# A graph layer on one core: edge lanes of 100000, an uneven last pair, last stores lane by lane, x loaded earlier, norm operands in PSUM

## The chip, the cores and the metric

One core of a Trainium2 chip runs the whole kernel. The time is the device time of one execution in microseconds (us), the median of several runs. Lower is better.

## The reference, cut to what matters

```python
h = maximum(layernorm(x), 0)                      # x: 12500 nodes x 32
e = concat([h[src], h[dst], edge_attr], -1)       # 400000 edges x 96, dst is sorted
v = relu(e @ W1 + b1) @ W2 + b2                   # 96 -> 64 -> 32
x_cand = segment_max(v, dst, num_segments=12500)
out = x + maximum(x_cand, h)
```

## The kernel before, in words

The 400000 edges are cut into A = 4 lanes. A lane lies on 32 partitions. A block is 32 x 16 = 512 edges of one lane, and a step of the main loop (a pair, `j`) takes two blocks of every lane. There are `PAIRS` = 98 pairs, which is 98 x 1024 = 100352 edges a lane (`LEN`), somewhat more than a quarter of the edges. So the lanes overlap: the first three start at equal distances (`STEP`), the last one at `E - LEN`. A load of edge attributes, first rows or mask is therefore two DMAs, one for three lanes and one for the fourth (`lanes_of`, `row_view`, L287 to L298, L356 to L366).

Ahead of the main loop ("the start", up to about 300 us) the kernel normalizes x (L799 to L820, on VectorE, with one square root on ScalarE), writes h to memory, searches the first edge of every node (TensorE L668 and L670, ScalarE L597), splits a table of h, and scatters h to the first edge of each node.

In a pair, 12 of each 16 rows of `h[src]` are fetched by GpSimd's indirect DMAs, one DMA for 128 rows: 24 gathers a pair (`gather_row`, L490). The other 4 of 16 are looked up by TensorE with one-hot matrices (L689). One-hots are made by VectorE (L927) and ScalarE (L615, L620). TensorE then runs the two layers (`layer_one`, `layer_two`, L704 to L727). VectorE turns inputs around (L958, L964, L969), spreads first rows over the edges with a scan (L973), takes the running maximum with a second scan (L984), turns it (L988), and SP stores it to `run_max` (L429).

What sets the order:
- SP's queue is in order. For a pair it waits and issues: edges for `j+2`, first rows for `j+2`, picks for `j+3`, every seventh pair the indices, then the mask for `j+2`, then the store of `j` (`feed`, L431 to L454). The wait ahead of the indices is on the gathers of the last pair of the running set of seven (L447).
- GpSimd gathers seven pairs ahead at most. Two gathers form a burst, and burst `b` of pair `j` waits until TensorE has used `(j - 5) * 13 + b` tiles (L507 to L511).
- VectorE's queue is in order: in `pair` it masks, turns edges, scans, makes one-hots, and last it turns the gathered rows of the next pair (`turn_src`, L954).

After the last pair SP loads x again, waits for all stores, and loads a row for each lane that carries a maximum over its border. GpSimd waits for all stores too, and then gathers one row of `run_max` for each node: 98 gathers (L560). VectorE joins them with h and x, and SP writes the output (L475).

Of the kernel before, what the change touches and what calls it, by code (L numbers as in the profile page):

```python
# [7 lines left out]
ALU = mybir.AluOpType  # L8
# [5 lines left out]
P = 128  # L14
# [5 lines left out]
A = 4  # L20
# [9 lines left out]
LEN = 2 * PAIRS * BLK  # L30
assert LANES == F == 32 and A * LEN >= E and PAIRS % (2 * AHEAD) == 0
STARTS = [a * ((E - LEN) // (A - 1)) for a in range(A - 1)] + [E - LEN]
STEPS = [STARTS[a] - STARTS[a - 1] for a in range(1, A)]
assert all(0 < s < LEN for s in STEPS)

STEP = STEPS[0]
assert STARTS[:-1] == [a * STEP for a in range(A - 1)]
LOADS = 2
# [5 lines left out]
PICKED = PICKS * LANES  # L44
WIDE = A * PICKED
# [3 lines left out]
BURSTS = 2 * GATHERS // BURST  # L49
assert BURSTS * BURST == 2 * GATHERS  # L50
# [58 lines left out]
STD_AT, WRITE_AT = 5, 7  # L109
# [12 lines left out]
def build(nc, x, src, dst, edge_attr, W1, b1, W2, b2, out):  # L122
    ctx = ExitStack()
    with ctx:
# [16 lines left out]
        run_max = dram("run_max", [A * LEN + 1, F])  # L141
# [26 lines left out]
        mean, var, std, rstd = (sb(n, [P, NJ]) for n in ("mean", "var", "std", "rstd"))  # L168
# [66 lines left out]

        ps_first = ps_layers[:, 2:4, :]
# [50 lines left out]
        def row_view(t, a0, a1):  # L287
            return bass.AP(t.tensor, STARTS[a0] * F, [[STEP * F, a1 - a0], [2 * R * F, LANES], [2 * BLK * F, PAIRS], [1, 2 * R * F]])

        def chunks(a0, a1):  # L290
            return slice(a0 * LANES, a1 * LANES)

        lanes_of = [(0, A - 1), (A - 1, A)]
        ea_view = [row_view(edge_attr, a0, a1) for a0, a1 in lanes_of]
        first_view = [row_view(first_rows, a0, a1) for a0, a1 in lanes_of]
        max_view = bass.AP(run_max.tensor, 0, [[LEN * F, A], [2 * R * F, LANES], [2 * BLK * F, PAIRS], [1, 2 * R * F]])
        ix_view = [bass.AP(src.tensor, STARTS[a], [[GATHERS, LANES], [BLK, 2 * PAIRS], [1, GATHERS]]).bitcast(U32) for a in range(A)]
        mask_view = [bass.AP(mask_dram.tensor, STARTS[a0], [[STEP, a1 - a0], [0, LANES], [2 * BLK, PAIRS], [1, 2 * BLK]]) for a0, a1 in lanes_of]  # L298
# [36 lines left out]
        def all_stored(eng):  # L335
            for s in range(2):
                eng.wait_ge(max_stored[s], D * (PAIRS // 2))
# [4 lines left out]
        def _(sp):  # L342
# [8 lines left out]
            def load_indices(j, half, loaded):  # L351
                for a in range(A):
                    sp.dma_start(src_ix[chunk(a), half, :, :, :].rearrange("l s g r -> l (s g) r"),
                                 ix_view[a][:, bass.ds(j * 2, 2 * AHEAD)]).then_inc(loaded, D)

            def load_edges(j, slot):  # L356
# [3 lines left out]
            def load_first(j, slot):  # L360
                for v, lanes in enumerate(lanes_of):
                    sp.dma_start(first_rows_in[chunks(*lanes), slot:slot + 1], first_view[v][:, :, bass.ds(j, 1)]).then_inc(first_loaded[slot], D)

            def load_mask(j, slot):
                for v, lanes in enumerate(lanes_of):
                    sp.dma_start(mask_rows_in[chunks(*lanes), slot:slot + 1], mask_view[v][:, :, bass.ds(j, 1)]).then_inc(mask_loaded[slot], D)  # L366
# [29 lines left out]
            sp.dma_start(run_max[A * LEN:A * LEN + 1, :], low_row[:, :]).then_inc(low_row_written, D)  # L396
# [29 lines left out]
            def store(j, slot):  # L426
                sp.wait_ge(max_turned, j * 2 + 2)
                sp.sem_inc(loads_begun, 1)
                sp.dma_start(max_view[:, :, bass.ds(j, 1)], max_rows[:, slot:slot + 1]).then_inc(max_stored[slot], D)  # L429

            def feed(j, k, turn, loads=True, picks=True, indices=True):  # L431
                slot = k % 2
                if loads:
                    sp.wait_ge(ea_turned, j * 2 + 2)
                    sp.sem_inc(loads_begun, 1)
                    load_edges(j + 2, slot)
                    sp.wait_ge(first_turned, j * 2 + 2)
                    sp.sem_inc(loads_begun, 1)
                    load_first(j + 2, slot)
# [4 lines left out]
                if indices and k % AHEAD == IX_AT:  # L444
# [4 lines left out]
                    load_indices(j + (2 * AHEAD - IX_AT), half, ix_loaded[half])  # L449
                if loads:  # L450
                    sp.wait_ge(max_scanned, j * 2 + 2)
                    sp.sem_inc(loads_begun, 1)
                    load_mask(j + 2, slot)
                store(j, slot)  # L454

            DOUBLE_TURNS = PAIRS // (2 * AHEAD)
            with sp.Fori(0, DOUBLE_TURNS - 1) as i:
                for k in range(2 * AHEAD):
                    feed(i * (2 * AHEAD) + k, k, i)
            for k in range(2 * AHEAD):  # L460
                j = (DOUBLE_TURNS - 1) * 2 * AHEAD + k
                feed(j, k, DOUBLE_TURNS - 1, loads=j + 2 < PAIRS, picks=j + 3 < PAIRS, indices=j + 2 * AHEAD - IX_AT < PAIRS)

            sp.wait_ge(tiles_used, PAIRS * TILES)
            sp.dma_start(x_again[0:PIECE], x_rows[0:PIECE]).then_inc(x_loaded, D)
            sp.dma_start(x_again[PIECE:P - 1], x_rows[PIECE:P - 1]).then_inc(x_loaded, D)
# [659 lines left out]
```

## Time and profile before

| what | value |
|---|---|
| median of 3 runs | 3253.02 us (3251.27 to 3254.14) |
| profiled execution, its own time | 3252.11 us |
| its span | 3250.3 us |
| mean granted TensorE clock, share of full | 0.967 |
| PE busy | 3011.4 us (93%) |
| POOL busy | 2432.8 us (75%) |
| DVE busy | 2193.5 us (67%) |
| ACT busy | 2108.6 us (65%) |
| DMA share of 16 engines, hardware queue / GpSimd's queue | 27.3% / 10.2% |

Busy time does not contain the time in which an engine's sequencer prepares its next instruction. On GpSimd this is 0.30 us ahead of each gather and counts as idle. DMA issues are shown for SP's queue as SPq; one row can stand for several issues. A time in a row is the start in us from the start of the span, then the duration. The last bracket is the idle time ahead of the instruction and what ended it.

### The profile page before, as it was taken

What the parts mean: (1) busy time and instruction counts of PE and PEld (TensorE: products, weight loads), DVE (VectorE), ACT (ScalarE), POOL (GpSimd) and SP (SyncE); (2) the same over time, 40 slices, a digit from 0 to 9 for tenths busy, and PEclk for the clock granted to TensorE, in tenths of its full rate; (3) what the DMA queues carried; (4) which work ended last, traced back from release to release, by engine and by line L of the source; (5) the groups of instructions that cost most, each with busy time, mean ns of one, the idle gap of its engine ahead of it and who ended that gap; (6) DMA issues with size and microseconds to landing.
All of it is one profiled execution on the core that took longest, in us unless ns stands there. A gap on an engine that the chain in (4) does not pass through costs nothing.

```text
span 3250.3 us, 56988 instructions
## 1 busy us (share of the span) xinstructions
PE 3011.4 (93%) x19600; PEld 2222.8 (68%) x19600; DVE 2193.5 (67%) x2408; ACT 2108.6 (65%) x2462; POOL 2432.8 (75%) x2558
## 2 busy tenths in 40 slices
PE   6999999999999999999999999999998998999800
PEld 4777677777777777777777777777676776777500
DVE  6221677777777777777777777777676767777623
ACT  2335677777777777777777777776775776777500
POOL 7777777777777777777777777777777777777746
PEclk9999999999999999999999999999999999999955
DMA  9940333333333333333333333333333333333211
GB/s 303 362 128 27 85 100 99 101 102 99 100 98 99 95 99 100 97 98 97 99 101 100 101 97 99 98 97 84 103 99 80 97 76 109 99 98 97 68 47 26
DMA packets 199047, 338.71 MB, mean 104 GB/s; under 512 B 78486, under 2 KB 122520, under 8 KB 198391
## 3 DMA queue, kind: packets, MB, share of 16 engines
q1 hardware_dynamic: 114866, 293.24, 27.3%
q0 software_dynamic: 81568, 41.91, 10.2%
q10 hardware_dynamic: 2464, 2.14, 0.2%
q14 instruction: 125, 1.02, 0.1%
q8 instruction: 24, 0.39, 0.0%
HBM read 228.49 MB, written 108.59 MB: 104 GB/s over the span
## 4 chain that ended last, share of the span: by engine, by line
PE 87%; DMA 4%; issue 3%; POOL 2%; DVE 2%; SPq 1%; ACT 0%; DVEq 0%; POOLq 0%; ACTq 0%
PE ps_rows L689 66%; PE ps_layers L668 4%; PE ps_layers L670 4%; PE ps_layers L704 3%; PE ps_layers L718 3%; PE ps_layers L727 3%; PE ps_layers L708 3%; PE ps_layers L713 2%; POOL gathered_max L560 2%; DMA picks<-picks_dram 2%; DMA gathered_max<-run_max,gather_ix 1%; POOL src_in L491 1%; DVE onehot L927 1%; DMA src_in<-h_dram,src_ix 0%; DMA dst_i<-in_dst_dram 0%
## 5 line engine op out<-in xcount | busy, mean ns | idle before, releaser
L491 POOL DMA_INDIRECT src_in<-h_dram,src_ix x2304 | 2176.7, 945 | 702.1 <-issue 638.4
L689 PE MATMUL ps_rows<-onehot,table 128*128 128x512 f32 x9800 | 2289.5, 393 | 21.7 <-DVE onehot L927 21.6
L689 PEld LDWEIGHTS ps_rows<-onehot,table 128*128 128x128 f32 x9800 | 1831.0, 188 | 495.9 <-issue 107.2
L620 ACT ACTIVATE onehot<-distance 128x1024 fp32r<-128x1024 bf16 x882 | 878.3, 1049 | 700.6 <-PE ps_rows L689 700.6
L615 ACT ACTIVATE distance<-picks,below_column 128x1024 bf16<-128x1024 int16 x882 | 954.8, 1136 | 52.2 <-DMA picks<-picks_dram 52.2
L927 DVE SCALAR_TENSOR_TENSOR onehot<-picks,column,ps_layers 128x1024 fp32r<-128x1024 int16 x392 | 493.1, 1279 | 365.2 <-PE ps_rows L689 339.0
L668 PE MATMUL ps_layers<-ea_t,rows_in 125*128 125x320 bf16 x980 | 269.1, 302 | 26.4 <-DVE rows_in L793 26.4
L969 DVE STREAM_TRANSPOSE ps_layers<-rows_in 128x512 f32<-128x512 f32 x196 | 129.4, 706 | 231.8 <-ACT hid L606 193.9
L670 PE MATMUL ps_layers<-dst_t,rows_in 125*128 125x320 bf16 x980 | 269.0, 301 | 0.0
L606 ACT ACTIVATE hid<-ps_layers,b_col 128x512 f32<-128x512 f32 x392 | 234.5, 675 | 40.2 <-PE ps_layers L718 40.2
L984 DVE TENSOR_TENSOR_SCAN max_t<-mask_in,max_t,ps_layers 128x512 f32<-128x512 bf16 x196 | 250.5, 1278 | 10.7 <-PE ps_layers L727 7.1
L973 DVE TENSOR_TENSOR_SCAN dst_t<-mask_in,dst_t,ps_layers 128x512 f32<-128x512 bf16 x196 | 251.0, 1281 | 7.0
L988 DVE STREAM_TRANSPOSE rows_in<-max_t 128x512 f32<-128x512 f32 x196 | 210.0, 1111 | 3.4
L945 DVE SCALAR_TENSOR_TENSOR picked_rows<-picks,fold,ps_rows 128x512 f32<-128x512 int16 x196 | 137.7, 744 | 107.8 <-PE ps_rows L689 107.8
L964 DVE STREAM_TRANSPOSE ea_t<-rows_in 128x512 f32<-128x512 f32 x196 | 195.3, 1078 | 0.0
L597 ACT ACTIVATE signs<-ps_layers,below_node 128x640 bf16<-128x640 f32 x98 | 77.7, 793 | 170.6 <-PE ps_layers L670 170.6
L958 DVE STREAM_TRANSPOSE src_t<-src_in 128x384 f32<-128x384 f32 x196 | 155.7, 870 | 16.3 <-DMA src_in<-h_dram,src_ix 16.2
L952 DVE COPY_PREDICATED picked_rows<-of_side,ps_rows 128x512 f32<-128x512 int16 x196 | 133.2, 735 | 18.1 <-DVE picked_rows L945 18.1
L704 PE MATMUL ps_layers<-ea_t,w_edge 32*64 32x512 f32 x1568 | 112.8, 632 | 30.7 <-DVE onehot L927 26.2
L668 PEld LDWEIGHTS ps_layers<-ea_t,rows_in 125*128 125x128 bf16 x980 | 96.3, 98 | 65.4 <-DVE rows_in L793 26.4
L560 POOL DMA_INDIRECT gathered_max<-run_max,gather_ix x98 | 92.5, 944 | 58.6 <-issue 55.2
L718 PEld LDWEIGHTS ps_layers<-picked_rows,w_src 128*64 128x64 f32 x1568 | 85.1, 139 | 61.5 <-DVE picked_rows L952 54.4
(108 smaller groups left out, 1107.1 us busy)
## 6 DMA issues: line engine op xcount, KB each, us to landing
picks<-picks_dram SPq DMA_DIRECT2D x98, 512.0 KB
run_max<-rows_in SPq DMA_DIRECT2D x98, 512.0 KB
first_rows<-hid SPq DMA_DIRECT2D x100, 500.0 KB
rows_in<-in_edge_attr_dram SPq DMA_DIRECT2D x98, 384.0 KB
rows_in<-first_rows SPq DMA_DIRECT2D x98, 384.0 KB
src_in<-h_dram,src_ix POOLq DMA_INDIRECT x2304
mask_in<-mask_dram SPq DMA_DIRECT2D x98, 192.0 KB
rows_in<-in_edge_attr_dram SPq DMA_DIRECT2D x98, 128.0 KB
```

Source lines behind the costliest of these rows:

```text
L491: pool.indirect_dma_start(out=src_in[:, slot, g, r, :], out_offset=None, in_=rows[:, :], in_offset=bass.IndirectOffsetOnAxis(ap=src_ix[:, ...
L606: nc.scalar.activation(hid[:, a, :], ps_hid[a][:, :], ACT.Relu, bias=b1_col[:, 0:1]).then_inc(hid_made, 1)
L615: nc.scalar.activation(distance[:, k, :], picks[:, slot, 0, :, :].rearrange("p g w -> p (g w)"), ACT.Abs, bias=below_column[:, i:i + 1]).t ...
L620: nc.scalar.activation(onehot[:, RING_AT[c] + BY_DVE[c] + k, :, :].rearrange("p g w -> p (g w)"), distance[:, k, :], ACT.Relu, bias=1.0, s ...
L668: nc.tensor.matmul(found[:, 0:HALF + half], begun, rise_hi[:, t, half * HALF:(half + 1) * HALF + half], start=t == 0, stop=False)
L670: mm = nc.tensor.matmul(found[:, 0:HALF], begun, rise_lo[:, t, half * HALF:(half + 1) * HALF], start=False, stop=t == BT - 1)
L689: mm = nc.tensor.matmul(ps_rows[g][side][:, 0:WIDE], table[:, i * SIDES + side, part, :], onehot[:, RING_AT[c] + t, g, :], start=(i + part ...
L704: nc.tensor.matmul(ps_hid[a][g * HID:(g + 1) * HID, :], w_edge[chunk(a), :], ea_t[chunk(a), slot, g, :], start=True, stop=False)
L927: compared = V.scalar_tensor_tensor(out=onehot[:, RING_AT[c] + t, :, :].rearrange("p g w -> p (g w)"), in0=picks[:, slot, 0, :, :].rearran ...
L973: V.tensor_tensor_scan(dst_t[:, slot, g, :], mask_in[:, slot, g, :], ps_first[:, g, :], dst_t[:, slot, 0, BLK - 1:BLK] if g else dst_t[:, ...
L984: V.tensor_tensor_scan(max_t[:, g, :], mask_in[:, slot, g, :], ps_v[g][:, :], max_t[:, 1 - g, BLK - 1:BLK], ALU.min, ALU.max).then_inc(max ...
L988: V.transpose(max_out[:, slot, h, :, :], of_half(max_t[:, :, :], h)).then_inc(max_turned, 1)
```

## The change

- A lane is exactly `LANE = E // A` = 100000 edges. Lanes no longer overlap, and all four start at equal distances. So each load of edges, first rows and mask is one DMA for four lanes instead of two.
- The last pair is short. A lane has `LAST` = 100000 - 97 x 1024 = 672 edges there: 21 rows of 32 edges in place of 32 rows. Its edges, first rows and stores are four DMAs, one for each lane. Its first block has 12 gathers, its second block has 1, so the pair has 13 gathers in place of 24. The matmul with gathered rows is narrower there for the second block (32 columns instead of 384).
- The last load of indices is eight DMAs (four more, of 32 single values each).
- SP's loop is one turn shorter, and two turns of 14 pairs are written out instead of one.
- The x that the end needs is loaded ahead of the store of pair 96, once TensorE has used all tiles, instead of behind the store of pair 97.
- The stores of pairs 96 and 97 are four DMAs each, one for each lane.
- In the norm of x, the mean and the reciprocal of the deviation are written to PSUM and read from there (L802, L805, L815, L817). The squares move from VectorE (L808) to ScalarE, ahead of its fourth item of the search.
- The positions of the rows that the end gathers need seven VectorE operations less, since lanes do not overlap (L995 to L1003). The picks of `src` are read by seven DMAs instead of four on ScalarE's queue.

```diff
-LEN = 2 * PAIRS * BLK
-STARTS = [a * ((E - LEN) // (A - 1)) for a in range(A - 1)] + [E - LEN]
+LANE = E // A
+STARTS = [a * LANE for a in range(A)]
+LAST = LANE - (PAIRS - 1) * 2 * BLK
+LAST_PARTS = LAST // (2 * R)
+LAST_GATHERED = LAST - BLK - PICKED
...
+        ps_mean, ps_rstd = (ps_rows[0][n][:, 0:NJ] for n in range(2))
...
+        def row_view(t):
+            return bass.AP(t.tensor, 0, [[LANE * F, A], [2 * R * F, LANES], [2 * BLK * F, PAIRS - 1], [1, 2 * R * F]])
+        def last_rows(t, start):
+            return bass.AP(t.tensor, (start + LANE - LAST) * F, [[2 * R * F, LAST_PARTS], [1, 2 * R * F]])
...
-                for v, lanes in enumerate(lanes_of):
-                    sp.dma_start(ea_rows[chunks(*lanes), slot:slot + 1], ea_view[v][:, :, bass.ds(j, 1)]).then_inc(ea_loaded[slot], D)
+            def load_edges(j, slot, last=False):
+                if last:
+                    for a in range(A):
+                        sp.dma_start(ea_rows[chunk_of_last(a), slot], last_rows(edge_attr, STARTS[a])).then_inc(ea_loaded[slot], D)
+                else:
+                    sp.dma_start(ea_rows[:, slot:slot + 1], ea_view[:, :, bass.ds(j, 1)]).then_inc(ea_loaded[slot], D)
...
+            def load_indices(j, half, loaded, last=False):
+                blocks = 2 * AHEAD - last
...
+                    if last:
+                        sp.dma_start(src_ix[chunk(a), half, AHEAD - 1, 1, 0:1], last_ix_view[a], allow_slow_non_contiguous=True).then_inc(loaded, D)
...
+            def store(j, slot, last=False, by_lane=False):
+                if last:
+                    for a in range(A):
+                        sp.dma_start(last_rows(run_max, STARTS[a]), max_rows[chunk_of_last(a), slot]).then_inc(max_stored[slot], D)
+                elif by_lane:
+                    for a in range(A):
+                        sp.dma_start(max_view[a][:, bass.ds(j, 1)], max_rows[chunk(a), slot:slot + 1]).then_inc(max_stored[slot], D)
...
+                if end:
+                    load_x()
+                store(j, slot, last, end)
...
+            def gather_pair(half, slot, tiles_before, last=False):
+                for b in range(BURSTS // 2 + 1 if last else BURSTS):
...
+                    if last and b == BURSTS // 2:
+                        gather_row(half, slot, 1, 0)
...
+                if j == SQUARE_AT:
+                    act.wait_ge(table_padded, 1)
+                    act.wait_ge(ln_step, 3)
+                    nc.scalar.activation(squared, centred, ACT.Square).then_inc(ln_step, 1)
...
-            V.tensor_tensor(centred, x_sb[:, :, :], mean[:, :].unsqueeze(2).broadcast_to([P, NJ, F]), ALU.subtract).then_inc(ln_step, 1)
-            V.tensor_tensor(squared, centred, centred, ALU.mult).then_inc(ln_step, 1)
+            V.tensor_tensor(centred, x_sb[:, :, :], ps_mean.unsqueeze(2).broadcast_to([P, NJ, F]), ALU.subtract).then_inc(ln_step, 1)
...
-                                   in1=rstd[:, :].unsqueeze(2).broadcast_to([P, NJ, F]),
+                                   in1=ps_rstd.unsqueeze(2).broadcast_to([P, NJ, F]),
```

## Rows read from the trace of the kernel before

**Rows 1.** The page, costliest groups: line engine op | busy, mean ns | idle.

```profile
L491 POOL DMA_INDIRECT src_in<-h_dram,src_ix x2304 | 2176.7, 945 | 702.1 <-issue 638.4
L620 ACT ACTIVATE onehot<-distance 128x1024 fp32r<-128x1024 bf16 x882 | 878.3, 1049 | 700.6 <-PE ps_rows L689 700.6
```

**Rows 2.** Waits of POOL: us in total, times, longest.

```profile
POOL src_in L491 <- PE ps_rows L689: 60.4, 198, 0.3
```

**Rows 3.** Timeline of POOL in the start.

```profile
32.35 3.68 POOL L491 DMA_INDIRECT src_in<-in_x_dram,src_ix  x1 [0.30 <-issue]
36.33 3.16 POOL L491 DMA_INDIRECT src_in<-in_x_dram,src_ix  x1 [0.30 <-issue]
39.79 0.94 POOL L491 DMA_INDIRECT src_in<-in_x_dram,src_ix  x1 [0.31 <-issue]
...
47.31 3.22 POOL L491 DMA_INDIRECT src_in<-in_x_dram,src_ix  x1 [0.30 <-issue]
```

**Rows 4.** Timeline of DVE and ACT in the start.

```profile
31.79 3.42 DVE L805 TENSOR_TENSOR work<-x_sb,mean 128x3136 f32<-128x3136 f32 x1
35.25 3.42 DVE L808 TENSOR_TENSOR work<-work 128x3136 f32<-128x3136 f32 x1
38.70 3.42 DVE L810 TENSOR_REDUCE var<-work 128x98 f32<-128x3136 f32 x1
...
46.29 3.43 DVE L817 SCALAR_TENSOR_TENSOR h_sb<-work,rstd 128x3136 f32<-128x3136 f32 x1
...
42.93 0.79 ACT L597 ACTIVATE signs<-ps_layers,below_node 128x640 bf16<-128x640 f32 x1 [1.79 <-PE ps_layers L670]
```

**Rows 5.** Timeline of POOL and PE, pair 7's second burst and pair 2's first tiles.

```profile
365.89 0.94 POOL L491 DMA_INDIRECT src_in<-h_dram,src_ix  x1 [0.30 <-PE ps_rows L689]
...
361.59 7.59 PE L689 MATMUL ps_rows<-onehot,table 128*128 128x512 f32 x32
```

**Rows 6.** Timeline of SP's queue, behind the last load of indices.

```profile
2672.16 1.90 SPq L353 DMA_DIRECT2D src_ix<-in_src_dram  x4
2674.32 1.57 SPq L366 DMA_DIRECT2D mask_in<-mask_dram  x2
```

**Rows 7.** The chain that ended last, in order of time.

```profile
2683.44 16.44 DMA picks<-picks_dram
...
2966.96 15.65 PE ps_rows L689 x68
...
2994.69 15.65 PE ps_rows L689 x68
...
3029.11 8.91 DMA src_in<-h_dram,src_ix
...
3085.06 10.04 DMA run_max<-rows_in
```

**Rows 8.** Timeline of all engines, last three pairs and the end.

```profile
3041.47 1.12 PE L704 MATMUL ps_layers<-ea_t,w_edge 32*64 32x512 f32 x16 [3.40 <-DVE onehot L927]
...
3089.02 0.94 POOL L491 DMA_INDIRECT src_in<-h_dram,src_ix  x1 [0.31 <-issue]
...
3084.74 1.96 PE L708 MATMUL ps_layers<-dst_t,w_dst 32*64 32x512 f32 x16
...
3095.30 0.84 DVE L958 STREAM_TRANSPOSE src_t<-src_in 128x384 f32<-128x384 f32 x1 [9.60 <-DMA src_in<-h_dram,src_ix]
...
3096.19 1.59 PE L713 MATMUL ps_layers<-src_t,w_src 32*64 32x384 f32 x16 [9.48 <-DVE src_t L958]
...
3105.76 2.00 DVE L988 STREAM_TRANSPOSE rows_in<-max_t 128x512 f32<-128x512 f32 x2
...
3118.98 0.94 POOL L560 DMA_INDIRECT gathered_max<-run_max,gather_ix  x1 [29.02 <-issue]
```

**Rows 9.** Stretches: us, busy PE, PEld, DVE, ACT, POOL, clock, DMA share, GB/s.

```profile
3088.00:3090.00 2.00, 0.00 (x0) 0.00 (x0) 0.00 (x0) 0.00 (x0) 1.66 (x2) 1.00 0.27 57
3111.00:3113.00 2.00, 0.00 (x0) 0.00 (x0) 0.00 (x0) 0.00 (x0) 0.00 (x0) 0.50 0.96 325
```

More of the change, by code:

```diff
@@ L29 @@
 TURNS = PAIRS // AHEAD
-LEN = 2 * PAIRS * BLK
-assert LANES == F == 32 and A * LEN >= E and PAIRS % (2 * AHEAD) == 0
-STARTS = [a * ((E - LEN) // (A - 1)) for a in range(A - 1)] + [E - LEN]
[L33 to L38, printed above, removed]
+LANE = E // A
+assert LANES == F == 32 and E == A * LANE and PAIRS % (2 * AHEAD) == 0 and PAIRS // (2 * AHEAD) > 2
+STARTS = [a * LANE for a in range(A)]
+LAST = LANE - (PAIRS - 1) * 2 * BLK
+LAST_PARTS = LAST // (2 * R)
 PICKS = 4
@@ L360, in load_first @@
[L360 to L366, printed above, removed]
+                    sp.dma_start(src_ix[chunk(a), half, :, :, :].rearrange("l s g r -> l (s g) r")[:, 0:blocks],
+                                 ix_view[a][:, bass.ds(j * 2, blocks)]).then_inc(loaded, D)
@@ L452, in feed @@
                     sp.sem_inc(loads_begun, 1)
-                    load_mask(j + 2, slot)
-                store(j, slot)
+                    load_mask(j + 2, slot, before_last)
+                if end:
+                    load_x()
+                store(j, slot, last, end)
             DOUBLE_TURNS = PAIRS // (2 * AHEAD)
-            with sp.Fori(0, DOUBLE_TURNS - 1) as i:
+            with sp.Fori(0, DOUBLE_TURNS - 2) as i:
                 for k in range(2 * AHEAD):
                     feed(i * (2 * AHEAD) + k, k, i)
[L460 to L466, printed above, removed]
-            sp.dma_start(x_again[P - 1:P, 0:TAIL], x_tail).then_inc(x_loaded, D)
-            sp.dma_start(x_again[P - 1:P, TAIL:NJ], x_fill).then_inc(x_loaded, D)
+            for turn in range(DOUBLE_TURNS - 2, DOUBLE_TURNS):
+                for k in range(2 * AHEAD):
+                    j = turn * 2 * AHEAD + k
+                    feed(j, k, turn, loads=j + 2 < PAIRS, picks=j + 3 < PAIRS, indices=j + 2 * AHEAD - IX_AT < PAIRS, end=j == PAIRS - 2,
+                         before_last=j == PAIRS - 3, last=j == PAIRS - 1, last_indices=j + 3 * AHEAD - IX_AT == PAIRS)
             all_stored(sp)
             for a in range(1, A):
-                sp.dma_start(carry[:, a - 1, :], bass.AP(run_max.tensor, ((a - 1) * LEN + STEPS[a - 1]) * F, [[0, P], [1, F]])).then_inc(carry_loaded, D)
+                sp.dma_start(carry[:, a - 1, :], bass.AP(run_max.tensor, (STARTS[a] - 1) * F, [[0, P], [1, F]])).then_inc(carry_loaded, D)
             for hb in range(1, NHB, 2):
@@ L505, in gather_early, with gather_turn @@
                     gather_burst(0, slot, b, x if slot < RAW_PAIRS else h_dram)
-            def gather_pair(half, slot, tiles_before):
-                for b in range(BURSTS):
+            def gather_pair(half, slot, tiles_before, last=False):
+                for b in range(BURSTS // 2 + 1 if last else BURSTS):
                     pool.wait_ge(tiles_used, tiles_before + b)
                     pool.sem_inc(gathers_begun, 1)
-                    gather_burst(half, slot, b)
-            def gather_turn(turn, half, loads):
+                    if last and b == BURSTS // 2:
+                        gather_row(half, slot, 1, 0)
+                    else:
+                        gather_burst(half, slot, b)
+            def gather_turn(turn, half, loads, last=False):
                 pool.wait_ge(ix_loaded[half], loads * (A * D))
@@ L519, in gather_turn @@
                     pool.sem_inc(gathers_begun, 1)
-                    gather_pair(half, slot, turn * (AHEAD * TILES) + (slot + 2 - AHEAD) * TILES)
+                    gather_pair(half, slot, turn * (AHEAD * TILES) + (slot + 2 - AHEAD) * TILES, last and slot == AHEAD - 1)
             pool.wait_ge(early_ix_loaded, A * D)
@@ L729, in layer_two, with pair @@
                 mm.then_inc(v_summed, 1)
-            def pair(j, slot, ahead=True):
-                layer_one(j, slot, ahead)
+            def pair(j, slot, ahead=True, last=False):
+                layer_one(j, slot, ahead, last)
                 if ahead:
@@ L748, in _ @@
             for slot in range(2):
-                pair(PAIRS - 2 + slot, slot, ahead=False)
+                pair(PAIRS - 2 + slot, slot, ahead=False, last=slot == 1)
         @block_.vector
@@ L1040, in _, with pair @@
             turn_edges(0, 0, 0)
-            def pair(j, k, turn, again, ahead=True, following=True):
+            def pair(j, k, turn, again, ahead=True, following=True, last_next=False):
                 slot = k % 2
```

125 lines of the change are left out of this document (67 added, 58 removed).

## The prediction

> **What bounds the kernel now.** The list of busy times points to TensorE with 93%, and the chain of waits gives it 87%. The waits of GpSimd say otherwise. I read the costliest groups first, then GpSimd's waits, then its timeline. 2304 gathers take 945 ns each, and the idle time ahead of each is the 0.3 us of its own sequencer [rows 1]. Where another engine is named for it, the longest wait is the same 0.3 us [rows 2]. So GpSimd issues a gather every 1.25 us from 5 us on and never really waits until its last gather at 3089.02 [rows 8]. A pair costs it 24 x 1.25 = 29.9 us. TensorE's undisturbed period is 27.7 us (2994.69 - 2966.96, the same look-ups of two pairs [rows 7]). GpSimd starts seven pairs ahead, loses 2.2 us a pair, and has used up its lead toward the end.
>
> That shows in three places. SP has to wait for gathers ahead of the load of indices. Its queue is in order, so mask, store, edges, first rows and picks come late behind it, and at three places of the chain (the last is shown) picks that land some 16 us after their issue end a wait [rows 7]. At the third last pair TensorE waits 3.40 us for a one-hot that stands in VectorE's queue behind a turn that waits for gathers which land 8.91 us after issue [rows 7, 8]. At the last pair TensorE waits 9.48 us for the last gather [rows 8]. Behind this the end is serial: turns, last store, 98 gathers on GpSimd, output.
>
> **The start.** Three gathers last 3.68, 3.16 and 3.22 us instead of 0.94 [rows 3]. Each lies inside one VectorE operation that reads two tiles of SBUF: the centring, the squares and the scaling [rows 4]. The reduction from 38.70 reads one, and the gather at 39.79 is of normal length. In the main loop VectorE's one-hots and masks all have an operand in PSUM, and the mean gather is 945 ns [rows 1]. The change gives the centring and the scaling an operand in PSUM and moves the squares to ScalarE. So GpSimd gains (3.68 - 0.94) + (3.16 - 0.94) + (3.22 - 0.94) = 7.2 us by 85 us; bounds 0 and 7.2.
>
> Most of it is lost again. Burst 1 of pair 7 may start only when TensorE has used one tile of pair 2. These four tiles run from 361.59 for 7.59 us [rows 5], so the first ends at 363.5; with 0.3 us for the sequencer the gather can start at 363.8. It starts at 365.89 now [rows 5]. So 2.0 us of the 7.2 survive; later bursts have more room.
>
> The squares on ScalarE: 1024 elements take 1.05 us and 640 take 0.79 [rows 1, 4]; that slope (0.7 ns an element) gives 2.5 us for 3136, one ns an element 3.3. I take 2.7. They start behind its third item at 38.4 and end at 41.1. Its fourth item then ends at 42.2, ahead of the 42.93 [rows 4] at which TensorE wants that buffer back. The variance comes 2.5 us later and so does the square root, and the item behind it still ends just ahead of its use. Cost 0; if one more table load is needed (1.28 us in the trace for the one before the root), up to 1 us of the search, which would leave 1 of the 2.0. The picks' extra DMAs on ScalarE's queue and the fewer VectorE operations for the places lie beside TensorE's first look-ups: 0. h is written 1.5 us later, at 58, and its first reader on GpSimd comes at 77 us: 0.
>
> **The main loop.** Gathers are as many as before until the last pair. SP issues three DMAs less a pair, which nobody waits for, because SP itself waits. Where it is late, two things count, and the last place (2672) is what remains in the result, since TensorE runs undisturbed from 2703 to 3038. First, from the first index DMA to the mask it is 2.16 us for four DMAs [rows 6]; now there are eight, at about 0.38 us each without register work: 3.0, so +0.9 (bounds 0 and 2.5). Second, the picks land at 2699.9 [rows 7], that is 25.6 us after the mask's issue, behind 500 KB on each of the busiest DMA engines. I get these by taking the three-lane DMA as three engines' work: 136 + 136 KB edges and first rows, 68 mask, 128 store, 32 picks. With four lanes in one DMA, on four engines, it is 480 KB: 25.6 x 20 / 500 = 1.0 us less. If more engines were used it would be up to 15 us less, if each engine slows with four at work up to 3 more. I take -1.0. The sum is 0.1 better, so TensorE comes to the third last pair 2.1 us earlier.
>
> There it still meets the gathers, which also come 2.0 us earlier. Their landing took 8.91 us with a store and 512 KB each of edges and first rows in flight. These last loads shrink to 344 KB and spread out; the landing lies between 2.4 us (what an undisturbed gather took ahead of 2672) and 8.9. With the store alone in flight it was 6.2 (3089.02 to 3095.2). The store starts before the gather in both cases, and its end fits both landings, so I take only 1.0 us. The bound is the whole stall with the clock's fall to half behind it: 3.4 + 1.7 = 5.1. Together 3.1 us by here, bounds 0 and 7.1.
>
> **The last pair.** Eleven gathers less: the last is issued at 3089.02 - 11 x 1.25 = 3075.3, and 2.0 earlier still. The load of x starts at about 3071 and could slow it; x moves at 325 GB/s [rows 9], so 1.57 MB are over some 7 us later. TensorE is ready for the gathered rows at 3084.74 + 1.96 = 3086.7 [rows 8], VectorE at 3085.9. So only 9.5 of the 13.7 us are gained: then TensorE's own order sets the end. The narrower matmuls take 0.6 off the 1.59 at L713. 10.1 us, bounds 5 and 10.8.
>
> **The last store.** VectorE's turn ends at 3107.76; GpSimd's first gather of the end is at 3118.98 [rows 8], 11.2 us later. In these the store lands, slowed by x. A store alone took 10.04 [rows 7] at 57 GB/s and a DMA share of 0.27, some 4.3 engines of 16 [rows 9]: one for each lane. A store of one lane has 21 rows as its slowest dimension; the x load with 112 rows reached a share of 0.96. The data of the last pair (344 KB) take 6.0 us at 57 GB/s, and 1.6 us if all 16 engines work at the same rate each. I take the middle, 3.8. With 0.6 to the first issue's end, 1.3 until data flow, 0.5 to the landing and 0.8 to GpSimd it is 7.0 instead of 11.2: 4.2 us, bounds 2 and 6.5. The store of pair 96 is over by then. The carried rows keep their distance to the store's landing, and 98 gathers at 1.25 us are unchanged.
>
> How many engines work is where a page bears. The Trainium skill, "DMA: Bandwidth & Descriptors", section on why a DMA increments its semaphore by 16, says that a DMA from SP uses the largest number up to 16 that divides the slowest dimension on both sides. The store's share of 0.27 agrees with 4. By it the lane's 21 rows get 7 engines, 3.7 us by the store's rate. By the same rule the merged loads get 4 engines and not 16, which speaks against any large gain in the main loop.
>
> **Sum.** 3.1 + 10.1 + 4.2 = 17.4 us. The span goes from 3250.3 to 3232.9, the profiled execution's time (1.8 above) to 3234.7, and with the median 0.9 above that execution, 3235.6.
>
> **Rivals.**
> 1. The gathers of the third last pair land without a stall. For: the loads beside them shrink. Against: the store's end explains both landings. 4.1 us more than taken, with a quicker store some 6: 3230. Chance 0.2.
> 2. The start gives nothing and costs: squares and a table load hold ScalarE longer than the room of one item, TensorE's search ends 2 us later, and with it burst 1 of pair 7. For: that room is 0.7 us by my count. 3.1 becomes 0.5: 3238. Chance 0.13.
> 3. The last gathers gain little: the load of x, ahead of two stores, holds their landing up until the last store but one is through, as the landings near stores were held up before. Then 10.1 becomes about 1: 3245. Against: they are issued 10 us ahead of that store. Chance 0.1.
> 4. The slower side: four lanes in one DMA make the busiest DMA engines the bound. Now they need 25.6 of 27.7 us a pair. From a 15% lower rate of each engine on, 480 KB take longer than a pair, and each of some 90 pairs would lose the excess; at 0.3 us, 3262. Against: each of these engines gets less to move than before, and only one more is as busy, where all 16 could work at a share of 0.96 with 325 GB/s [rows 9]. Chance 0.05.
>
> **How the numbers follow.** The forecast has 0.52, with 3231 to 3240 of its own. The range reaches to rivals 1 to 3: 3226 to 3246. No change is within 0.2%, 6.5 us, about what a measurement can tell. Faster holds the forecast, rivals 1 and 2 and a part of 3: 0.89; same 0.06; slower 0.05.
>
> **What would show it.** No gather near 32, 36 and 47 us above 1 us. GpSimd pausing at pair 7 for about 5 us. Picks behind the last late load of indices landing 25 us after the mask's issue. Last pair: no wait at L713, GpSimd done before TensorE. End: 7 us from VectorE's last turn to GpSimd's first gather of `run_max`. I am wrong if TensorE's period leaves 27.7 us, or if GpSimd waits anywhere else in the loop.

## The result, and the profile after

In the comparison of the two kernels the changed one takes 3234.59 us (median of 6 runs, 3231.48 to 3237.9) and the one before 3252.18 (median of 6, 3251.27 to 3254.5): a ratio of 0.9944, 95% interval 0.9933 to 0.9955, 0.6% faster. The forecast was 3235.6. The profiled execution took 3233.21, its span went from 3250.3 to 3231.1: 19.2 us, where the sum of the prediction was 17.4. Eleven of the twelve experiments ran on machines on which a pair takes about 40 us, not 27.7. Each is compared only with runs of the kernel before of its own group, on the same chip. The times are medians of all runs, but the ratios are of fast runs alone, those not over 1.5% above the fastest of their kernel, so a ratio can differ from the quotient of two medians.

From the page after, the span, the busy times and the costliest group (columns as in [rows 1]):

```profile
span 3231.1 us, 56108 instructions
PE 3004.2 (93%) x19600; PEld 2220.7 (69%) x19600; DVE 2190.1 (68%) x2400; ACT 2111.4 (65%) x2463; POOL 2417.3 (75%) x2547
L523 POOL DMA_INDIRECT src_in<-h_dram,src_ix x2293 | 2170.7, 947 | 703.4 <-issue 634.7
```

The waits of GpSimd after (line waited for: us in total, times, longest). The longest wait for TensorE was 0.3 us [rows 2] and is 5.1 now, a single one:

```profile
POOL src_in L523 <- issue: 649.0, 2130, 0.3
POOL src_in L523 <- PE ps_rows L733: 65.1, 198, 5.1
```

The timeline after (start us, length, engine, line, what; in brackets the idle time before it and what ended it), the rows that answer to [rows 3 to 6, 8]:

```profile
32.11 3.42 DVE L849 TENSOR_TENSOR work<-x_sb,ps_rows 128x3136 f32<-128x3136 f32 x1
32.62 0.94 POOL L523 DMA_INDIRECT src_in<-in_x_dram,src_ix  x1 [0.30 <-issue]
...
38.37 2.83 ACT L627 ACTIVATE work<-work 128x3136 f32<-128x3136 f32 x1
41.09 0.79 ACT L641 ACTIVATE signs<-ps_layers,below_node 128x640 bf16<-128x640 f32 x1
...
47.59 0.94 POOL L523 DMA_INDIRECT src_in<-in_x_dram,src_ix  x1 [0.30 <-issue]
...
361.59 7.55 PE L733 MATMUL ps_rows<-onehot,table 128*128 128x512 f32 x32
364.48 0.94 POOL L523 DMA_INDIRECT src_in<-h_dram,src_ix  x1 [5.09 <-PE ps_rows L733]
...
2671.58 0.33 SPq L360 DMA_DIRECT2D src_ix<-in_src_dram  x1
2675.68 0.57 SPq L383 DMA_DIRECT2D mask_in<-mask_dram  x1
2702.93 1.12 PE L747 MATMUL ps_layers<-ea_t,w_edge 32*64 32x512 f32 x16 [3.71 <-DVE onehot L968]
2706.51 5.74 PE L733 MATMUL ps_rows<-onehot,table 128*128 128x512 f32 x24
...
2997.78 0.58 SPq L454 DMA_DIRECT2D run_max<-rows_in  x1
3008.49 0.86 DVE L1003 STREAM_TRANSPOSE src_t<-src_in 128x384 f32<-128x384 f32 x1 [7.15 <-DMA src_in<-h_dram,src_ix]
3011.93 2.01 PE L747 MATMUL ps_layers<-ea_t,w_edge 32*64 32x512 f32 x16 [3.94 <-DVE onehot L968]
...
3058.39 0.58 SPq L454 DMA_DIRECT2D run_max<-rows_in  x1
3068.29 0.86 DVE L1003 STREAM_TRANSPOSE src_t<-src_in 128x384 f32<-128x384 f32 x1 [6.01 <-DMA src_in<-h_dram,src_ix]
3075.01 0.94 POOL L523 DMA_INDIRECT src_in<-h_dram,src_ix  x1 [0.30 <-issue]
3081.03 2.01 PE L747 MATMUL ps_layers<-ea_t,w_edge 32*64 32x512 f32 x16 [5.39 <-DVE max_t L1029]
3083.10 1.72 SPq L452 DMA_DIRECT2D run_max<-rows_in  x4
3084.50 1.50 PE L757 MATMUL ps_layers<-src_t,w_src 32*64 32x384 f32 x16
3093.12 2.01 DVE L1033 STREAM_TRANSPOSE rows_in<-max_t 128x512 f32<-128x512 f32 x2
3095.23 1.41 SPq L449 DMA_DIRECT2D run_max<-rows_in  x4
3098.96 1.31 SPq L503 DMA_DIRECT2D carry<-run_max  x3
3099.65 0.94 POOL L596 DMA_INDIRECT gathered_max<-run_max,gather_ix  x1 [23.69 <-issue]
```

The reader is to see four things. In the start, gathers issued inside the centring (32.62) and inside the scaling (47.59) are of normal length. At pair 7 GpSimd now stands still. The last gather is 14.0 us earlier than in [rows 8], and nothing ends a wait at L757, where 9.48 us stood. From VectorE's last turn to the first gather of `run_max` it is 3099.65 - 3095.13 = 4.52 us, where it was 11.22.

The loads at 3098.96 wait for all stores. From the chain that ended last (start us, length, what; it answers to [rows 7]):

```profile
2678.61 21.36 DMA picks<-picks_dram
...
2998.83 9.64 DMA src_in<-h_dram,src_ix
...
3084.40 3.47 DMA run_max<-rows_in
```

The stretches while the store of pair 96 (the first) and the last store move (columns of [rows 9]):

```profile
3084.00:3086.00 2.00, 2.00 (x26) 0.39 (x19) 0.00 (x0) 0.00 (x0) 0.00 (x0) 0.50 0.92 242
...
3096.00:3097.00 1.00, 0.00 (x0) 0.00 (x0) 0.00 (x0) 0.45 (x1) 0.00 (x0) 0.50 0.46 131
3097.00:3098.00 1.00, 0.00 (x0) 0.00 (x0) 0.00 (x0) 0.00 (x0) 0.00 (x0) 0.50 0.41 143
```

### The profile page after: what moved, and what is told of

It is laid out like the page before. It is cut to its first block, busy times and chain, and to the rows that moved or that the text cites. A ratio compares the mean times of both kernels' runs of the same rounds, so it can differ in the third digit from the quotient of the medians.

```text
span 3231.1 us, 56108 instructions
## 1 busy us (share of the span) xinstructions
PE 3004.2 (93%) x19600; PEld 2220.7 (69%) x19600; DVE 2190.1 (68%) x2400; ACT 2111.4 (65%) x2463; POOL 2417.3 (75%) x2547
## 4 chain that ended last, share of the span: by engine, by line
PE 87%; DMA 4%; POOL 3%; issue 2%; DVE 2%; SPq 1%; ACT 0%; POOLq 0%; DVEq 0%; ACTq 0%
PE ps_rows L733 66%; PE ps_layers L712 4%; PE ps_layers L714 4%; PE ps_layers L747 3%; PE ps_layers L762 3%; PE ps_layers L771 3%; PE ps_layers L751 3%; DMA picks<-picks_dram 2%; POOL gathered_max L596 2%; PE ps_layers L757 2%; POOL src_in L523 1%; DMA gathered_max<-run_max,gather_ix 1%; DVE onehot L968 1%; DMA src_in<-h_dram,src_ix 1%; DMA dst_i<-in_dst_dram 0%
## 5 line engine op out<-in xcount | busy, mean ns | idle before, releaser
L714 PE MATMUL ps_layers<-dst_t,rows_in 125*128 125x320 bf16 x980 | 268.8, 301 | 0.0
L1003 DVE STREAM_TRANSPOSE src_t<-src_in 128x384 f32<-128x384 f32 x195 | 154.7, 871 | 13.2 <-DMA src_in<-h_dram,src_ix 13.2
L747 PE MATMUL ps_layers<-ea_t,w_edge 32*64 32x512 f32 x1568 | 111.9, 627 | 29.2 <-DVE onehot L968 23.8
```

Source lines behind the costliest of these rows:

```text
L714: mm = nc.tensor.matmul(found[:, 0:HALF], begun, rise_lo[:, t, half * HALF:(half + 1) * HALF], start=False, stop=t == BT - 1)
L747: nc.tensor.matmul(ps_hid[a][g * HID:(g + 1) * HID, :], w_edge[chunk(a), :], ea_t[chunk(a), slot, g, :], start=True, stop=False)
```

## The experiments

The theory is that of the prediction: GpSimd's gathers bound the kernel, and the gain is made of gathers left out, a shorter last store and a little at the start. The rivals tested are that the start is not what it seems, that the early load of x makes the end shorter, and that stores by lane would end the slow landings.

**The normalization alone.** To the kernel before only the part on the normalization is added:

```diff
-            V.tensor_scalar(mean[:, :], mean[:, :], 1.0 / F, None, ALU.mult).then_inc(ln_step, 1)
+            V.tensor_scalar(ps_mean, mean[:, :], 1.0 / F, None, ALU.mult).then_inc(ln_step, 1)
...
-            V.tensor_tensor(squared, centred, centred, ALU.mult).then_inc(ln_step, 1)
...
+                    nc.scalar.activation(squared, centred, ACT.Square).then_inc(ln_step, 1)
```

> The kernel before with only the norm part of the change (operands in PSUM, squares on ScalarE). Theory (GpSimd sets the pace, but its lead is cut by the wait for tiles at pair 7): no gather over 1.2 us near 32, 36 and 47 us; a pause of about 5 us at pair 7; from there every gather 1.4 to 2 us earlier than before; time 1 to 2 us less, 3250.5 to 3252. Rival (the lead is kept): last gather 6 to 7 us earlier, time 3245 to 3246. Rival (the start is of no account): last gather where it was, 3252.

Measured: 4391.89 us against 4410.86, ratio 1.0024 (0.998 to 1.0067): no difference can be told. The machine was of the kind with a pair of some 40 us, so the time says nothing on the 2.0 us. The gathers of the start can be read all the same. The centring runs at 31.86 to 35.28 here, but the scaling only at 70.88, not at 46. Timeline of GpSimd and VectorE in this kernel:

```profile
32.37 0.94 POOL L493 DMA_INDIRECT src_in<-in_x_dram,src_ix  x1 [0.30 <-issue]
...
70.88 3.42 DVE L820 SCALAR_TENSOR_TENSOR h_sb<-work,ps_rows 128x3136 f32<-128x3136 f32 x1
73.40 0.94 POOL L493 DMA_INDIRECT src_in<-in_x_dram,src_ix  x1 [2.06 <-PE ps_layers L676]
```

Beside the centring, the squares and the scaling stood 3.68, 3.16 and 3.22 us [rows 3]. Now the gathers beside centring and scaling take 0.94, and the squares are no longer on VectorE. So the part on the normalization alone removes the long gathers: shown, though no trace of the kernel before exists from such a machine. What became of the pause of 5 us at pair 7 can't be told here, where GpSimd waits for TensorE in many places. What the machine is like is in the waits of this kernel and in a stretch of it:

```profile
POOL src_in L493 <- PE ps_rows L695: 694.5, 337, 41.8
PEld ps_layers L714 <- issue: 593.6, 553, 2.7
PE ps_layers L714 <- issue: 250.1, 292, 2.3
...
600.00:2600.00 2000.00, 1771.36 (x9218) 1156.63 (x9224) 1051.39 (x1076) 1060.89 (x1127) 1161.30 (x1228) 0.89 0.27 71
```

The same stretch of the kernel before, on a machine where a pair takes 27.7 us:

```profile
600.00:2600.00 2000.00, 1976.81 (x12782) 1466.59 (x12781) 1481.99 (x1492) 1456.80 (x1563) 1511.81 (x1603) 1.00 0.37 98
```

12782 matmuls there, 9218 here, where a pair takes 39.2 us (the same product of two pairs at 999.39 and 1038.61). Here TensorE and its weight loads stand between the narrow products of L714, ended by nothing that the profile shows, and GpSimd waits for TensorE, up to 41.8 us. So GpSimd is not the bound there, and a test of what bounds the other machine can't be made by its total time. A later expectation says that TensorE stood for instructions there; no trace shows for what it stood.

It was run once more in a second group of runs, on another chip.

> Again, where GpSimd is the bound: the kernel before with only the norm part. Theory (the lead won in the start is cut at pair 7): three gathers of normal length, GpSimd waits some 5 us for tiles at pair 7, last gather 1.4 to 2 us earlier than 3089.0, time 1 to 2 us less, 3250 to 3251.5. Rival (the whole lead is kept): last gather at 3082, time 3245 to 3246. Rival (no effect): 3252.2.

4389.49 against 4382.56, ratio 1.0009 (0.9977 to 1.0041): again no difference can be told, under the same limit.

**x loaded behind the last store.** From the changed kernel:

```diff
-                if end:
-                    load_x()
                 store(j, slot, last, end)
...
+            load_x()
             all_stored(sp)
```

> The changed kernel with the load of x put back behind the last store; the stores stay lane by lane. From VectorE's last turn to GpSimd's first gather of run_max it is 4.5 us in the changed kernel and 11.2 in the one before. Theory (both edits share the gain, x's 1.57 MB slow the landing): some 3 to 5 us come back, 7.5 to 9.5 us there, time 3 to 5 us over the changed kernel, 3237.5 to 3239.5. Rival (the gain is all from the stores by lane): 4.5 to 5 us there, time as the changed kernel, 3234.6. Rival (all from x): 11 us there, 3241.

Measured: 4417.74 against 4410.86, ratio 1.008 (1.0041 to 1.0119); it tells nothing on 3 to 5 us. But the distance from the last turn to the first gather of `run_max` doesn't hang on the pairs before. Timeline of the end of this kernel:

```profile
4273.69 1.99 DVE L1032 STREAM_TRANSPOSE rows_in<-max_t 128x512 f32<-128x512 f32 x2
4275.78 1.42 SPq L449 DMA_DIRECT2D run_max<-rows_in  x4
4277.24 0.33 SPq L459 DMA_DIRECT2D x_again<-in_x_dram  x1
...
4280.23 0.94 POOL L595 DMA_INDIRECT gathered_max<-run_max,gather_ix  x1 [175.95 <-issue]
```

4280.23 - 4275.68 = 4.55 us, as with x loaded early (4.52). In the normalization-only kernel of the same machine, with a whole last store, the distance is 4262.38 - 4251.14 = 11.24. My expectation that a late load of x costs some us of it falls: all of the gain at the last store comes from its form and size, with four DMAs of 21 rows in place of one of 128 rows.

**All gathers of the last pair.** The changed kernel, but with the 11 gathers kept:

```diff
-                for b in range(BURSTS // 2 + 1 if last else BURSTS):
+                for b in range(BURSTS):
...
-                        dve.wait_ge(src_gathered[k % AHEAD][g], turn * (2 * D * GATHERS) + (k // AHEAD) * (D * GATHERS) + D)
+                        dve.wait_ge(src_gathered[k % AHEAD][g], turn * (2 * D * GATHERS) + (k // AHEAD + 1) * (D * GATHERS))
```

> The changed kernel with 24 gathers in the last pair again; the eleven added ones fetch rows that nobody uses, and VectorE waits for them. Nothing else differs. Theory (GpSimd's issue rate sets when the last rows arrive): last gather issued 11 x 1.25 = 13.7 us later, near 3088.7; TensorE waits 8 to 11 us at the matmul with gathered rows of the last pair again; time 8 to 12 us over the changed kernel, 3243 to 3246. Rival (TensorE or the shorter last loads gave the gain, not the gathers): less than 3 us over it.

Measured: 4435.3 against 4410.86, ratio 1.0109 (1.0012 to 1.0206). Timeline of its last pair:

```profile
4318.92 1.50 PE L754 MATMUL ps_layers<-src_t,w_src 32*64 32x384 f32 x16
...
4334.21 0.94 POOL L593 DMA_INDIRECT gathered_max<-run_max,gather_ix  x1 [173.29 <-issue]
```

No wait for the last gather, although all 24 are there: the last one was issued at 4159.98, 159 us before this product. The 8 to 11 us that the theory expected did not come. That gathers cost nothing where GpSimd is far ahead fits the theory; that the eleven are worth 9.7 us where it is behind is not shown by this run. Repeated twice:

> Again, as on the first chip TensorE was the bound (a pair took some 40 us and GpSimd waited for it): the changed kernel with 24 gathers in the last pair. Theory (GpSimd's issue rate sets when the last rows arrive): last gather some 13.7 us later than the changed kernel's 3075.0, TensorE waits 8 to 11 us at the matmul with gathered rows of the last pair, time 8 to 12 us over the changed kernel, 3243 to 3246. Rival (the shorter last loads or TensorE's own order gave the gain): less than 3 us over it.

4450.68 against 4382.56, ratio 1.017 (1.0123 to 1.0217).

> The changed kernel with 24 gathers in the last pair, now for a chip on which a pair takes 27.7 us. Theory (GpSimd's issue rate sets when the last rows arrive): last gather near 3088.7, TensorE waits 8 to 11 us at the matmul with gathered rows of the last pair; ratio to the kernel before 0.997 to 0.998, where the changed kernel has 0.994. Rival (the shorter last loads or TensorE's own order gave the gain): 0.994 to 0.995.

4348.11 us; in this group the runs of the kernel before went from 4314.39 to 4466.49 (median 4442.62), so there is no ratio. All three are inconclusive on the eleven gathers.

**All stores by lane.** The changed kernel with every store as four DMAs, one a lane:

```diff
...
-                elif by_lane:
+                else:
                     for a in range(A):
                         sp.dma_start(max_view[a][:, bass.ds(j, 1)], max_rows[chunk(a), slot:slot + 1]).then_inc(max_stored[slot], D)
-                else:
-                    sp.dma_start(max_view[:, :, bass.ds(j, 1)], max_rows[:, slot:slot + 1]).then_inc(max_stored[slot], D)
...
```

> The changed kernel with every store of the loop as four DMAs, one for each lane, as the last two are. In the changed kernel a store takes about 10 us on the four busiest DMA engines (480 KB a pair on each), gathers that are issued while one runs land 9 to 10 us after issue and hold VectorE's queue once near the end (3.9 us at TensorE plus 1.4 us at half clock), and picks behind a late load of indices land 24.3 us after the mask. Theory (a gather's landing waits for a store that is in flight on the same engines): stores over 16 engines take 3 to 4 us, no gather lands later than 6 us, the stall in the last pairs goes, picks land 6 us sooner; time 3 to 8 us under the changed kernel, 3227 to 3232. Rival (the loads, not the stores, hold gathers up): landings stay at 9 us and the time stays at 3234.6. Rival (12 more issues a pair load SP, whose queue becomes late everywhere): slower than the changed kernel.

4436.77 against 4410.86, ratio 1.0125 (1.0062 to 1.0187).

> Again, where GpSimd is the bound: the changed kernel with every store of the loop lane by lane. Theory (a gather issued while a store is in flight lands only when the store has landed): no gather lands later than 6 us, no stall over 1 us at a turn of gathered rows in the last five pairs, picks behind the last late load of indices land 17 to 20 us after the mask instead of 24.3; time 3 to 8 us under the changed kernel, 3227 to 3232. Rival (loads hold gathers up): landings of 9 us stay, 3234.6. Rival (SP is late with 12 issues more a pair): slower.

4446.64 against 4382.56, ratio 1.0165 (1.013 to 1.02).

> The changed kernel with every store of the loop lane by lane, where a pair takes 27.7 us. Theory (a gather issued while a store is in flight lands only when the store has landed): landings at turns of gathered rows under 6 us, no stall at such a turn, picks behind the last late load of indices 17 to 20 us after the mask; ratio to the kernel before 0.992 to 0.993, 3 to 8 us under the changed kernel. Rival (loads hold gathers up): landings of 9 us stay, 0.994.

4378.89, no ratio. Gathers are far ahead of their turns in these runs, so a landing that waits for a store delays nobody, and the question stays open.

**Edges, first rows and stores by lane.** The loads of edges and first rows are cut in four as well:

```diff
-                    sp.dma_start(ea_rows[:, slot:slot + 1], ea_view[:, :, bass.ds(j, 1)]).then_inc(ea_loaded[slot], D)
+                    for a in range(A):
+                        sp.dma_start(ea_rows[chunk(a), slot:slot + 1], ea_view[a][:, bass.ds(j, 1)]).then_inc(ea_loaded[slot], D)
...
```

> As stores_by_lane, and the loads of edges and first rows lane by lane too, so that they spread over more than four DMA engines. Theory (what is left of TensorE's stalls behind a late load of indices is the queue of the four busy engines): picks land 5 to 9 us after the mask, those stalls of some 15 us vanish, but GpSimd's rate still sets the last pairs, so the time is only 0 to 3 us under that with stores by lane. Rival (the stalls themselves cost): 10 us or more under it. Rival (28 issues a pair on SP): slower.

4399.74 against 4382.56, ratio 1.0044 (1.002 to 1.0068).

> Stores, edges and first rows lane by lane, where a pair takes 27.7 us. Theory (GpSimd's rate sets the last pairs, TensorE's stalls further up cost nothing of themselves): picks 5 to 9 us after the mask, the stalls of some 15 us behind late loads of indices vanish, and yet the time is only 0 to 3 us under that with stores by lane. Rival (those stalls cost): 10 us or more under it, 3215 to 3222. Rival (28 issues a pair on SP): slower.

4288.85 (4283.56 to 4303.14), no ratio. In both groups it is below the kernel that stores by lane and loads four lanes at once, by 1.1% (4446.64) and 2.1% (4378.89). On these machines the form of the loads counts; why is open, and no run tells what it would do with a pair of 27.7 us. So no version that beats both kernels was shown.

**The changed kernel again.** Without an edit, on another chip, to have a second profile.

> The changed kernel once more, beside the kernel before on the same chip. On the two chips of the last runs both took some 4400 us: a pair took about 40 us because TensorE stood for instructions, GpSimd waited for TensorE, and the kernels derived from the changed one were 0.4 to 1.7% slower than the one before. Theory (the gain is GpSimd's, so it goes where TensorE is the bound, and only the 6.7 us of the last store stay): on such a chip the ratio is 0.998, 7 us less; on a chip where a pair takes 27.7 us it is 0.994 to 0.995. Rival (two turns of SP's loop written out, or loads merged on four engines, cost there): ratio 1.005 to 1.015 on such a chip.

This machine was of the kind of the result: 3237.5 us (4 runs, 3234.33 to 3238.61) against 3256.62 (7 runs, 3254.39 to 3258.26), ratio 0.9938 (0.9921 to 0.9954). The gain is repeated. The span is 3236.5, 5.4 longer than in the first profile after, and the timeline and a stretch (us, busy PE, clock, DMA share, GB/s) tell where that is from:

```profile
361.00:364.00 3.00, 3.00 (x40) 0.56 0.51 171
...
364.10 7.56 PE L733 MATMUL ps_rows<-onehot,table 128*128 128x512 f32 x32
367.00 0.94 POOL L523 DMA_INDIRECT src_in<-h_dram,src_ix  x1 [7.33 <-PE ps_rows L733]
...
3080.03 0.95 POOL L523 DMA_INDIRECT src_in<-h_dram,src_ix  x1 [0.30 <-issue]
...
3090.66 0.92 PE L757 MATMUL ps_layers<-src_t,w_src 32*64 32x384 f32 x16
3098.44 1.99 DVE L1033 STREAM_TRANSPOSE rows_in<-max_t 128x512 f32<-128x512 f32 x2
...
3104.95 0.94 POOL L596 DMA_INDIRECT gathered_max<-run_max,gather_ix  x1 [23.97 <-issue]
```

The tiles of pair 2 start 2.51 us later than in the first profile after. Of this 0.87 us was there before: the products ahead of them start at 358.88 and not 358.01, and TensorE's first look-up at 302.51 and not 301.37. The other 1.64 us are the clock's: soon after a wait of 2.19 us for a one-hot the granted clock fell, and over 361 to 364 us its mean is 0.56, near the lower level of 1.2 GHz. GpSimd's restart at pair 7 is 2.52 us later. From there to the last gather it waits nowhere and takes 2713.03 us for the same 2170 steps, 2.50 more. Together it is 5.02 us late at the last gather. TensorE gets the lateness too, by way of the last late load of indices (2676.15, was 2671.58), and VectorE's last turn ends 5.3 us later. The other signs are the same: one pause at pair 7, no wait at L757, 3104.95 - 3100.43 = 4.52 us at the last store.

## Why the prediction held, point by point

**GpSimd bounds the loop: right.** After the pause at pair 7 it never waits until 3075.01, and the second profile shows the same; a delay at that pause is found again at the last gather, 2713 us later. On machines where GpSimd is not the bound, the gain is gone (ratios 1.0044 to 1.017 for the kernels derived from the changed one, which did not run there itself). This fits the theory but is no clean test: a lost gain would give a ratio of about 1, and these kernels are slower than the one before, so something in them costs time there. The rivals named for it, two turns of SP's loop written out and four lanes in one DMA, are not told apart by any run; that cutting the loads by lane wins 1.1 and 2.1% there points at the second. That the eleven gathers gave the gain of the last pair rests on the traces alone.

**The start: the mechanism right, with 1.4 us for 2.0, and little of it lasts.** No gather is stretched, the pause is 5.09 us ("about 5"), and the gather behind it comes at 364.48, where the prediction had 363.8. Against [rows 5] that is 1.41 us. I had the first tile end at 363.5 and the gather 0.3 us later; it is 1.0 us later. At the last late load of indices (2671.58, was 2672.16) GpSimd's lead is down to 0.6 us, as its steps were longer. The squares take 2.83 us on ScalarE (2.7 taken), with no further table load, and TensorE's first look-up is at 301.37 against 301.25 (302.51 in the second profile, so about 1 us of this differs between executions). Rival 2 is out. The Trainium skill, "SBUF — State Buffer", section on who interferes with whom, says that a VectorE instruction with two SBUF inputs contends with a GpSimd one that reads SBUF and that the second to issue is blocked. The traces agree: 3.68 us beside a centring with two SBUF tiles, 0.94 beside one with its mean in PSUM. The gathers do not lie inside one VectorE operation, as I wrote; they begin inside it and end 0.8 us behind its end (36.03 behind 35.21, 39.49 behind 38.67, 50.53 behind 49.72), so each stood until the operation was over.

**The main loop: 0.1 better was taken, it came out 0.7 worse, and luck made up for it.** From the first index DMA to the mask it is 4.10 us and not 3.0, since each of the eight costs 0.51 and not 0.38: 1.9 us lost where 0.9 was taken. The picks land at 2699.97, 24.3 us behind the mask's issue (24.6 taken, 25.6 before): 1.3 us won where 1.0 was taken. With the lead of 0.6 us the picks land when they landed before (2699.88), where the prediction had TensorE 2.1 us earlier. Rival 4 is out: the busiest DMA engines got no slower, and TensorE's period stayed at 27.7 us. What I had not counted is the clock. TensorE's waits for the one-hot end nearly together (2702.93, before 2702.82), but the products behind take 1.12 and not 2.01 us, and the look-ups go on at 2706.51 and not 2708.86: 2.35 us. Timeline of TensorE before, at this place, and the stretch behind the wait, before and then after (columns of [rows 9]; the clock is the last but two):

```profile
2702.82 2.01 PE L704 MATMUL ps_layers<-ea_t,w_edge 32*64 32x512 f32 x16 [4.35 <-DVE onehot L927]
...
2708.86 3.47 PE L689 MATMUL ps_rows<-onehot,table 128*128 128x512 f32 x14
...
2703.00:2705.00 2.00, 2.00 (x24) 0.75 (x30) 1.84 (x4) 2.00 (x3) 1.47 (x2) 0.50 0.28 87
...
2703.00:2705.00 2.00, 2.00 (x41) 1.01 (x48) 1.84 (x4) 2.00 (x3) 1.64 (x2) 1.00 0.34 119
```

Before, the engine had stood for 4.35 us and the granted clock was at the lower level; after, it had stood for 3.71 us and the clock was still at the upper one. In the second profile after, behind a wait of 2.69 us, the products of L747 and L751 take 1.50 and 2.07 us at this place. So this differs between executions of one kernel, and I do not put it down to the change.

**The third last pair: the stall was rightly kept, but it moved, and it got no cheaper.** It now falls one pair earlier (3.94 us at 3011.93, none at 3041.15) and once, at 3068.29, beside the path. In the second profile it is where it was, a gather of 3033.78 landing after 8.42 us. By the last look-ups (they begin at 3044.79, before at 3046.76) TensorE is 1.97 us earlier; 3.1 were forecast for start, loop and stall. But of the 2.35 us that it was ahead at 2706.51 the stall took 0.4, where it was to give 1.0. So the 1.97 us are the clock's; up to the picks start and loop together gave nothing. That this step came near its forecast is luck.

**The last pair: the mechanism right, with some luck in the size.** VectorE's last turn ends 3107.76 - 3095.13 = 12.63 us earlier; less the 1.97 it is 10.66, where 10.1 was forecast. Up to the products of L757 it is 11.69 - 1.97 = 9.72 (9.5 forecast). The narrower matmuls, taken at 0.6, gave 0.1: the product behind L757 starts 1.43 us after it (3085.93), before 1.52. The rest is L771 at 1.09 us for 1.96, with a granted clock of 1.00 (3088 to 3090) for 0.50 (3101 to 3103 before): luck again. Rival 3 is out: no wait for the last gather is left, although it was issued at 3075.01, while x was loaded (3069 to 3077).

**The last store: the mechanism right, the size too small, and outside its bounds.** 6.70 us instead of 4.2 (bounds 2 to 6.5). I had taken 3.8 us for the data of the last pair, at a rate between 4 and 16 engines, and 3.2 us for what lies before and behind it. In the last store the DMA share is 0.46 and 0.41 at 131 and 143 GB/s: some 7 of 16 engines, about 19 to 20 GB/s each, where the whole store had 57 GB/s at 0.27, about 13 each. The rule of the Trainium skill, "DMA: Bandwidth & Descriptors", section on why a DMA increments its semaphore by 16, that the prediction cited gives 7 for 21 rows, and the share agrees. The lanes of pair 96, of 32 rows, have a share of 0.92 at 242 GB/s, some 15 engines. But the price that I worked out for 7, 3.7 us, supposed 13 GB/s an engine. At 131 GB/s and more the 344 KB are over in about 2.5 us, which leaves 2.0 of the 4.52 us for the rest: data move from 3096 on (share 0.46), before the last of the four issues ends at 3096.64. Most of the gain is the form and not the size. The store of pair 96 has all 512 KB, cut by lane, and lands 3087.87 - 3083.10 = 4.77 us behind its first issue, its last lane 3.47 us behind its own, where the whole store took 10.04. The last one, at 344 KB, takes 3098.96 - 3095.23 = 3.7. As the experiment with the late x shows, x had no part in it.

**The sum.** 1.97 + 10.66 + 6.70 = 19.3 us, against 3.1 + 10.1 + 4.2 = 17.4; the span gave 19.2, since the 98 gathers to the end take 131.45 and not 131.32. By these terms 1.1 us too little went one way, 0.6 (last pair) and 2.5 (last store) too much the other. Without what the clock gave, 2.35 and 0.9 us, the three would be about 16 (an estimate). So the forecast is near in part because errors cancel; but the two steps that it names as the main ones, gathers left out at the last pair and a quicker last store, hold 9.7 + 6.7 = 16.4 of the 19.3.

**What stays open.** The landings of gathers beside a whole store fit the store's end in each of five cases: 3038.02 behind a store issued at 3027.50; 3095.1 behind one issued at 3085.06 [rows 7]; 3008.47 behind 2997.78, 3068.3 behind 3058.39, and in the second profile 3042.20 behind 3031.93. That is 9.9 to 10.7 us behind the store's issue, where a store alone took 10.04 and an undisturbed gather 2.4. But a gather does not always wait for the store's end. By the semaphore updates in the trace of the kernel before, the gather issued at 1096.32 landed at 1101.6, while the store issued just ahead of it, at 1096.24, landed at 1106.4. So in its strict form the explanation is out, and what sets these landings stays open: the runs that would have told it met machines on which nobody waits for those landings.

## What to carry to other kernels

An engine with 75% busy time can be the bound if it goes without a pause; then its work is worth its full price only until the next engine's own order takes over (9.7 of 13.7 us at the last pair), and its gains in the start only up to the next point where it catches up with its buffers (1.4 of 7.2, and 0.6 at the last late load of indices). Where a serial end hangs on one store, cut it into DMAs that more engines work on. Check that the machine of an experiment has the same bound as the one of the result before a total is read, and have a second profile of the same kernel at hand: here two differ by 5.4 us.

## What the runs showed of the hardware that I had not expected

- Two kinds of machine: the same kernel before took 3252 and 3257 us on some, and 4383 to 4443 (medians) on others. In a trace from one of these, TensorE stands between narrow products with nothing named as the cause, 250 us in all at one line, and its weight loads there 594 us.
- A DMA engine moved about 13 GB/s in a store of 128 rows as one DMA and about 19 to 20 GB/s in one of four times 21 rows.
- GpSimd's step from gather to gather is not a constant: 1.2486 us before, 1.2491 and 1.2502 in the two profiles after (2723.13 us for 2181 steps, 2710.53 and 2713.03 for 2170). Over the loop this is 1.1 and 3.6 us.
- Behind a wait of 3.71 us TensorE was still granted its upper clock, behind one of 4.35 us in another execution the lower: 1.12 or 2.01 us for the same 16 matmuls.
- A gather issued beside a VectorE operation with two SBUF tiles ended 0.8 us behind the end of that operation, three times of three.
